# Delta-rule stage of a two-layer decoder kernel: projections and first taps issued ahead of exponentials and transposes

## The chip, the cores and the metric

One core of one Trainium2 chip runs the whole program in one launch. The metric is device time in microseconds (us); lower is better. Engines are named as in the profile: PE is TensorE (matmuls and transposes), ACT is ScalarE, DVE is VectorE, POOL is GpSimd, SP is SyncE, which here issues most DMAs. Each engine runs its own instructions strictly in the order written and waits on semaphores.

## The reference, cut to what matters

The program is a decoder of two layers, each an attention, a cross attention and a mixture. The change lies in one of the six stages, the attention of layer 1, a gated delta rule with 12 heads of 128 (keys, queries) and 32 (values), over 4 sequences of 256 tokens:

```python
q = short_conv(hidden_states @ Wq, conv_wq)     # 4 taps along time, then silu
k = short_conv(hidden_states @ Wk, conv_wk)
v = short_conv(hidden_states @ Wv, conv_wv)
q = l2norm(q.reshape(B, T, H, -1)); k = l2norm(k.reshape(B, T, H, -1))
beta = jax.nn.sigmoid(hidden_states @ Wb)
g = -jnp.exp(A_log) * jax.nn.softplus(hidden_states @ Wa + dt_bias)
# per head, step by step over t:
S = S * jnp.exp(gt); delta = (vt - kt @ S) * bt
S = S + kt[:, None] * delta[None, :]; o = qt @ S
o_n = o * rsqrt(mean(o * o) + eps) * norm_w * silu(hidden_states @ Wg)
return o_n.reshape(B, T, -1) @ Wo
```

The kernel computes the recurrence in two chunks of 128 tokens for each sequence: decay matrices E from cumulated g, products of keys with keys and queries, the inverse of a unit triangular matrix per chunk (first in blocks of 16, then doubled by matmuls), and the state carried from the first chunk to the second.

## The kernel before

`delta_attention` is written by hand with semaphores. Each engine has one loop `for i in span`, i from -1 to 14; I call one pass of it a step. In step i the heads overlap as in a pipeline:

- head a = i+1: its four projections `project(a, 0..3)` on PE (keys for two pairs of sequences, then queries) into the two PSUM banks of `dh_pj`; the first tap of the convolution, `tap0`, on ACT (L1909); the other three, `taps`, on DVE (L2170); `silu` on ACT (L1917) into `dh_back` and `dh_silu`. For the decays: `mask_g` on POOL (L2389), `segment` on PE (L1630), `exp` on ACT (L1921), `mask_e` on POOL (L2399).
- head b = i: `turn(b, 0..3)` transposes on PE (L1642), `copy_k0` (L1926) and `square` (L1931) on ACT, `sums` and scales `d` (L2176 to L2189) on DVE, `scale_e` on POOL (L2350), `k_products` on PE (L1654), `weigh` on DVE (L2205, L2207).
- head i-3: the levels of the inverse (`level4_x` L1670 up to `level6_y` L1719). They read blocks that POOL has solved (`solve`, L2370 and L2372, for two heads at a time in the even steps from 2 on) and that SP takes through DRAM: `dh_Tm` out to `delta_t`, `delta_t` back to `dh_U`. From i = 3.
- head i-4: the chain `solution` (L1735), `state`, `within` (L1753), `carried`. From i = 4.
- steps -1 to 3 also compute v for all heads: `project_v` on PE, `taps_v` on ACT (L1875, 4 instructions of 128x512), `conv_v` on POOL (L2407, 3 instructions), `silu_v`, `turn_v`, `copy_v`. Steps 11 and 12 compute the output gates (`gate`, L1562).

Buffers set the cross waits: `turn(b, 0)` shares a bank of `dh_tp` with `segment(b, 0)`, so it waits for `exp(b, 0)`; `turn(b, 2)` waits for all of `silu(b, ...)` and for `square(b, 0)`; `project` waits for the taps that read its bank. On ACT the exponentials use another function table than silu, so each step has two table loads; a dummy activation, `early` (L2063), brings the silu table back right behind the exponentials.

Of the kernel before, what the change touches and what calls it, by code (L numbers as in the profile page):

```python
# [1339 lines left out]
def delta_attention(nc, env, first, lf, latent, a, blk_a, blk_t, blk_tt):  # L1340
# [6 lines left out]
    with ExitStack() as ctx:  # L1347
# [88 lines left out]
        UO = (0, 32, 0, 32)  # L1436
        span = range(-1, D_H - 1 + LAG_CHAIN)
        ab, dec = bd[:, 0, 0:TILES * 2 * D_H].rearrange("p (t h) -> p t h", t=TILES), bd[:, 1, 0:2 * TILES * D_H].rearrange("p (n x) -> p n x", n=2)
        v_units, v_turns = {-1: (0, 1), 0: (2, 3), 1: (4, 5)}, {1: (0, 1), 2: (2, 3), 3: (4, 5)}
        spare = [x[:].rearrange("p t (n i) -> p (t n i)", n=1) for x in (PT[3], PT[4], AT[3])]  # L1440
        tap_v = lambda n, j: spare[j - 1][:, 512 * (n % 2):512 * (n % 2) + 512].rearrange("p (b t) -> p b t", t=SEQ)
# [3 lines left out]
        with nc.Block() as block:  # L1445
# [75 lines left out]
            def _(pe):  # L1521
# [95 lines left out]
                def project(a, n):  # L1617
                    u, (m, s) = 4 * a + n, divmod(n, 2)
                    if n == 0:
                        pe.wait_ge(w_loaded[a % 2], 32 * (a // 2 + 1))  # L1620
                    need(pe, tapped, 3 * (u - 1))
                    for k in range(KC):
                        mm = pe.matmul(pj[:, n % 2, :], w[a % 2][:, m, k, :], env.xT[:, k, 512 * s:512 * s + 512], start=(k == 0), stop=(k == KC - 1))  # L1623
                    mm.then_inc(projected, 1)
# [143 lines left out]
                for i in span:  # L1768
                    a, b = heads(i + 1), heads(i)
                    news, olds, late, ends = v_units.get(i, ()), v_turns.get(i, ()), gates.get(i, ()), outs.get(i, ())  # L1770
                    if b is not None:
                        turn(b, 0)
                        turn(b, 1)
                    if a is not None:
                        project(a, 0)
                    if i == -1:
                        betas_and_gates()
                    for h in chain_heads(i):
                        solution(h, 0)
                    for l in level_heads(i):  # L1780
                        level4_x(l)
                    for t in late[0:1]:
                        gate(t)
                    if b is not None:
                        turn(b, 2)
                        turn(b, 3)
                    if a is not None:
                        project(a, 1)
                    for n in olds[0:1]:
                        turn_v(n)  # L1790
                    for n in news[0:1]:
                        project_v(n)
                    for q in ends[0:1]:
                        turn_pair(q)
                    for l in level_heads(i):
                        level4_y(l)
                    for h in chain_heads(i):
                        state(h)
                    for t in late[1:2]:
                        gate(t)  # L1800
                    if b is not None:
                        k_products(b, 0)
                        k_products(b, 1)
                    for l in level_heads(i):
                        level5_x(l)
                    for h in chain_heads(i):
                        within(h, 0)
                    for h in chain_heads(i):
                        carried(h)
                    for q in ends[0:1]:  # L1810
                        out_pair(q)
                    for l in level_heads(i):
                        level5_y(l)
                    for h in chain_heads(i):
                        turn_carried(h)
                    if a is not None:
                        project(a, 2)
                    for n in olds[1:2]:
                        turn_v(n)
                    for n in news[1:2]:  # L1820
                        project_v(n)
                    for t in late[2:3]:
                        gate(t)
                    for q in ends[1:2]:
                        turn_pair(q)
                    for h in chain_heads(i):
                        solution(h, 1)
                    for l in level_heads(i):
                        level6_x(l)
                    if b is not None:  # L1830
                        k_products(b, 2)
                        k_products(b, 3)
                    for t in late[3:4]:
                        gate(t)
                    for q in ends[1:2]:
                        out_pair(q)
                    for l in level_heads(i):
                        level6_y(l)
                    for h in chain_heads(i):
                        within(h, 1)  # L1840
                    if i == -1:
                        decays()
                    if a is not None:
                        segment(a, 0)
                        segment(a, 1)
                        project(a, 3)
                for f in range(2):
                    turn_last(f)
                for f in range(2):
# [5 lines left out]
            def _(act):  # L1855
# [63 lines left out]
                def exp(a, c):  # L1919
                    act.wait_ge(seg_done, 2 * a + c + 1)  # L1920
                    act.activation(E[a % 2][c][:], tp[:, c, :].rearrange("p (b i) -> p b i", b=BATCH), ACT.Exp).then_inc(exp_done, 1)  # L1921
# [68 lines left out]
                for i in span:  # L1990
# [4 lines left out]
                    if b is not None:  # L1995
                        copy_k0(b)
                        square(b, 0)
                        square(b, 1)
                    if a is not None:
                        tap0(a, 0)  # L2000
                    if i == -1:
                        act.wait_ge(z_done, 1)
                        act.activation(u_[:], u_[:], ACT.Exp, scale=-1.0).then_inc(u_done, 1)
                        act.activation(par[:, :, B_, :], ab[:, :, 0:D_H].rearrange("p t h -> p h t"), ACT.Sigmoid).then_inc(beta_done, 1)
                    if b is not None:
                        silu(b, 3)
                    for l in level_heads(i):
                        copy_x4(l)
# [49 lines left out]
                    if i == -1:  # L2058
                        exp_decays()
                    if a is not None:  # L2060
                        exp(a, 0)
                        exp(a, 1)
                        act.activation(early[:], env.c("ident")[:, 0:1], ACT.Silu)  # L2063
                        tap0(a, 3)
                    for n in news[1:2]:
                        taps_v(n)
                for f in range(D_H - 2, D_H):
                    square_out(f)
                for f in range(2):
# [273 lines left out]
            def _(pool):  # L2343
# [83 lines left out]
                for i in span:  # L2427
                    a, b, g, f = heads(i + 1), heads(i), group(i), heads(i - LAG_NORM)
                    news = v_units.get(i, ())
                    if b is not None:  # L2430
                        scale_e(b, 0)
                        scale_e(b, 1)
                    if g is not None:
                        eye(g)
                        if g < PAIRS - 1:
                            solve(g)
                            turn_solved(g)
                    if i == D_H:
                        pool.wait_ge(x6_done, 9)
                        pool.memset(AT[0][:], 0.0).then_inc(recleared, 1)  # L2440
                        pool.wait_ge(o_done, 16)
                        pool.memset(PT[2][:, :, 0:64], 0.0).then_inc(recleared, 1)
                    for l in level_heads(i):
                        if l % 4 == 0:
                            pool.wait_ge(v_copied, 2 * (l // 4) + 2)
                        rhs(l)
                    if i == -1:
                        pool.wait_ge(g_done, 1)
                    if a is not None:
                        mask_g(a, 0)  # L2450
                        mask_g(a, 1)
                    for n in news[0:1]:
                        conv_v(n)
                    if b is not None:
                        if i == 0:
                            pool.wait_ge(dec_exp, 1)
                        norms(b)
                    if f is not None:
                        invert_out(f)
                        if f < 8:  # L2460
                            norm_out(f)
                    if a is not None:
                        mask_e(a, 0)
                        mask_e(a, 1)
                    for n in news[1:2]:
                        conv_v(n)
                for f in range(D_H - 2, D_H):
                    invert_out(f)
                pool.wait_ge(half_done, 1)
# [970 lines left out]
```

## Time and profile before

| What | Value |
|---|---|
| median of 3 runs | 1415.07 us (1415.04 to 1422.34) |
| the profiled execution | 1407.76 us, of which the profile's span is 1405.8 us |
| delta stage in the span | 461.9 us to about 860 us |
| busy over the span | PE 91%, DVE 58%, ACT 39%, POOL 37% |
| mean granted TensorE clock | 0.935 of 2.4 GHz |
| step length, first tap to first tap (L1909, last of each step), steps 0 to 4 | 23.9, 24.4, 27.2, 23.7, 25.3 us |
| the same, steps 5 to 10 | 25.3 to 25.4 us each |

The busy share of one engine over the whole span hides that stages differ; the stretches of single steps below are the ones to read. "Idle before" in a row is how long the engine stood still before that row, and the arrow says what ended the wait. A PE row gives the modelled length of its matmuls; the next row's start is the better measure of how long PE was held.

### The profile page before, as it was taken

What the parts mean: (1) busy time and instruction counts of PE and PEld (TensorE: products, weight loads), DVE (VectorE), ACT (ScalarE), POOL (GpSimd) and SP (SyncE); (2) the same over time, 40 slices, a digit from 0 to 9 for tenths busy, and PEclk for the clock granted to TensorE, in tenths of its full rate; (3) what the DMA queues carried; (4) which work ended last, traced back from release to release, by engine and by line L of the source; (5) the groups of instructions that cost most, each with busy time, mean ns of one, the idle gap of its engine ahead of it and who ended that gap; (6) DMA issues with size and microseconds to landing.
All of it is one profiled execution on the core that took longest, in us unless ns stands there. A gap on an engine that the chain in (4) does not pass through costs nothing. (4 is left out here: it accounts for less than half of the span.)

```text
span 1405.8 us, 25099 instructions
## 1 busy us (share of the span) xinstructions
PE 1272.7 (91%) x9172; PEld 842.6 (60%) x9172; DVE 813.6 (58%) x1826; ACT 548.4 (39%) x1273; POOL 523.1 (37%) x597
## 2 busy tenths in 40 slices
PE   7999999847896877999999977799999989999998
PEld 4868778635555444677777766345555555344487
DVE  5464655556354475676776423577777773743343
ACT  4554636233223576767667331144344351000010
POOL 3452627530751367476577301322222201500010
PEclk9999999958898798999999977899999999999999
DMA  3010038533886201212122120100000206542100
GB/s 132 24 37 15 22 108 277 202 125 148 237 251 200 79 11 24 43 31 40 34 38 26 20 43 1 62 20 21 21 22 30 63 1 172 180 139 68 34 8 23
DMA packets 144168, 106.57 MB, mean 76 GB/s; under 512 B 87873, under 2 KB 130089, under 8 KB 142913
## 3 DMA queue, kind: packets, MB, share of 16 engines
q1 hardware_dynamic: 135904, 88.31, 22.0%
q0 software_dynamic: 4496, 13.33, 3.6%
q10 hardware_dynamic: 3664, 3.55, 0.8%
q8 instruction: 66, 1.08, 0.3%
q14 instruction: 38, 0.30, 0.1%
HBM read 84.16 MB, written 22.35 MB: 76 GB/s over the span
## 5 line engine op out<-in xcount | busy, mean ns | idle before, releaser
L2811 PE MATMUL la_banks<-la_xe,la_f_w 128*128 128x512 f32 x348 | 151.4, 593 | 3.5 <-DVE la_xe L3189 3.5
L2170 DVE SCALAR_TENSOR_TENSOR dh_front<-dh_pj,df_conv,dh_front 128x510 f32<-128x510 f32 x144 | 107.4, 746 | 76.2 <-ACT dh_front L1909 72.4
L3352 POOL TENSOR_TENSOR la_area<-la_area 128x512 f32<-128x512 f32 x48 | 60.3, 1277 | 172.4 <-DVE la_area L3032 152.0
L2811 PEld LDWEIGHTS la_banks<-la_xe,la_f_w 128*128 128x128 f32 x348 | 65.4, 190 | 83.6 <-issue 83.6
L346 POOL TENSOR_TENSOR wa_qkT<-lf_area 128x512 f32<-128x512 f32 x40 | 50.7, 1268 | 96.8 <-DVE lf_area L318 96.8
L3189 DVE TENSOR_TENSOR la_xe<-xT,la_area 128x1024 f32<-128x1024 f32 x29 | 52.6, 1830 | 55.5 <-PE la_banks L2811 48.1
L2929 ACT ACTIVATE la_area<-la_banks,la_nmax 128x256 f32<-128x256 f32 x128 | 59.0, 475 | 58.5 <-DVE la_nmax L3041 58.5
L350 POOL TENSOR_TENSOR mw_gu<-mw_gu,const 128x384 f32<-128x384 f32 x64 | 63.6, 999 | 30.0 <-ACT mw_gu L381 30.0
L3372 POOL TENSOR_TENSOR la_o_rstd<-la_o_var,la_minus_half 128x1 f32<-128x1 f32 x8 | 6.4, 803 | 164.3 <-DVE la_o_var L3251 164.3
L2937 ACT COPY la_area<-la_banks 128x512 f32<-128x512 f32 x64 | 37.5, 590 | 56.2 <-PE la_banks L2660 55.9
L273 PE MATMUL wa_po<-wa_wo,mw_rows 128*128 128x256 f32 x256 | 56.6, 379 | 0.0
L2864 PE MATMUL la_banks<-la_y,la_area 128*128 128x256 f32 x256 | 56.2, 379 | 0.0
L3041 DVE TENSOR_REDUCE la_nmax<-la_banks 128x4 f32<-128x1024 f32 x32 | 39.1, 1221 | 26.9 <-PE la_banks L2646 26.7
L2864 PEld LDWEIGHTS la_banks<-la_y,la_area 128*128 128x128 f32 x256 | 48.4, 190 | 6.9 <-issue 0.5
L1623 PE MATMUL dh_pj<-xT,df_w 128*128 128x512 f32 x96 | 49.7, 643 | 2.9 <-PEq L133 2.9
L273 PEld LDWEIGHTS wa_po<-wa_wo,mw_rows 128*128 128x128 f32 x256 | 48.0, 190 | 6.2
L3052 DVE TENSOR_SCALAR la_area<-la_area,la_rec 128x256 f32<-128x256 f32 x128 | 50.3, 454 | 1.1
L318 DVE TENSOR_TENSOR lf_area<-wa_swap,const 128x512 f32<-128x512 f32 x40 | 48.4, 1209 | 0.0
L2613 PE MATMUL la_banks<-xT,lf_area 128*128 128x512 f32 x96 | 45.5, 616 | 2.5 <-PEq L133 2.5
L1623 PE MATMUL dh_pj<-xT,dh_w 128*128 128x512 f32 x96 | 46.7, 609 | 0.0
L2613 PE MATMUL la_banks<-xT,la_area 128*128 128x512 f32 x96 | 44.8, 602 | 0.0
L2660 PEld LDWEIGHTS la_banks<-const,la_area 128*128 128x128 f32 x256 | 28.6, 141 | 25.2 <-issue 22.7
(621 smaller groups left out, 3090.1 us busy)
## 6 DMA issues: line engine op xcount, KB each, us to landing
mw_gu<-in_L_ffn_gate_up SPq DMA_DIRECT2D x16, 768.0 KB, 14.2
placed<-mw_rows SPq DMA_DIRECT2D x8, 768.0 KB, 10.7
mw_d<-in_L_ffn_down SPq DMA_DIRECT2D x16, 384.0 KB, 13.6
mw_rows<-placed SPq DMA_DIRECT2D x8, 768.0 KB, 6.8
la_area<-w_table POOLq DMA_DIRECT2D x6, 1024.0 KB, 12.2
pairs<-me_picked SPq DMA_DIRECT2D x7, 704.0 KB, 3.9
la_f_w<-in_L_ffn_q_proj SPq DMA_DIRECT2D x32, 128.0 KB, 2.2
la_f_w<-in_L_ffn_k_proj SPq DMA_DIRECT2D x32, 128.0 KB, 2.4
```

Of the source, the lines that this page charges most:

```text
L273: mm = pe.matmul(po[:, (t + 1) % 2, 0:DIM], encT[:, i, P * t:P * t + P], wos[:, i, :], start=(i == 0), stop=(i == A_G - 1))
L346: pool.tensor_tensor(qkT[:, m, 512 * c:512 * c + 512], t_cos[:, n % 2, :], t_sin[:, n % 2, :], ALU.add).then_inc(rotated, 1)
L350: pool.tensor_tensor(masked[:, u % 3, :], probs[:, u % 2, :], env.c("a_mask"), ALU.mult).then_inc(mask_done, 1)
L1623: mm = pe.matmul(pj[:, n % 2, :], w[a % 2][:, m, k, :], env.xT[:, k, 512 * s:512 * s + 512], start=(k == 0), stop=(k == KC - 1))
L2170: dve.scalar_tensor_tensor(dst, src[:, :, 0:SEQ - j], conv[:, a, m, D_CONV - 1 - j:D_CONV - j], dst, ALU.mult, ALU.add).then_inc(tapped, 1)
L2613: mm = pe.matmul(qb[:, n, :], wabs[i % 2][:, k, n, :], env.xT[:, k, 512 * c:512 * c + 512], start=(k == 0), stop=(k == KC - 1))
L2811: mm = pe.matmul(acc[c][m], f_w[n % SLOTS][:, m, k, :], xe[(n - U) % RING][:, k, :], start=first and k == 0, stop=last and k == KC - 1)
L2864: mm = pe.matmul(o_acc[t % 4], ae[t % RING][:, x, :], f_wo[:, x, :], start=(x == 0), stop=(x == F_E - 1))
L2929: ins = act.activation(e[:, u % 2, a, n, :], sc[bank(j, b)][:, a, n, :], ACT.Exp, bias=nmax[:, a, t:t + 1], accum_out=total[:, a, t:t + 1])
L3052: ins = dve.tensor_scalar(en[:, u % 2, a, n, :], e[:, u % 2, a, n, :], rec[:, a, 2 * b + n:2 * b + n + 1], None, ALU.mult)
L3189: dve.tensor_tensor(xe[(n - U) % RING][:], env.xT[:, :, HALF * c:HALF * c + HALF], wb[c][:, x:x + 1, :].to_broadcast([P, KC, HALF]), ALU.m ...
L3352: pool.tensor_tensor(qrot[:, c, n, :], prod[:, c, 2 * n, :], prod[:, c, 2 * n + 1, :], ALU.add).then_inc(rotated, 1)
```

## The change

Nothing is added or removed; instructions change place on PE, ACT and POOL; DVE and SP keep their order.

- PE: `project(a, 0)` now comes before `turn(b, 0)` and `turn(b, 1)`; `project(a, 3)` before the two `segment`s.
- ACT: `tap0(a, 3)` comes before the two `exp`s. In steps 0 to 2 (`filling`) `silu(b, 3)` comes before `tap0(a, 0)`; later steps keep it behind. The second `taps_v` of a step moves from its end into the next step, behind `tap0(a, 0)`.
- POOL: the second `conv_v` of a step moves into the next step, behind `scale_e`. In step 2 (`g == 0`) `mask_g` comes before the solve.

```diff
+        filling = lambda i: i < LAG_LEVELS
...
 # PE
+                    if a is not None:
+                        project(a, 0)
                     if b is not None:
                         turn(b, 0)
                         turn(b, 1)
-                    if a is not None:
-                        project(a, 0)
...
                     if a is not None:
+                        project(a, 3)
                         segment(a, 0)
                         segment(a, 1)
-                        project(a, 3)
...
 # ACT
                         square(b, 0)
                         square(b, 1)
+                    if b is not None and filling(i):
+                        silu(b, 3)
                     if a is not None:
                         tap0(a, 0)
+                    for n in v_units.get(i - 1, ())[1:2]:
+                        taps_v(n)
...
-                    if b is not None:
+                    if b is not None and not filling(i):
                         silu(b, 3)
...
                     if a is not None:
+                        tap0(a, 3)
                         exp(a, 0)
                         exp(a, 1)
                         act.activation(early[:], env.c("ident")[:, 0:1], ACT.Silu)
-                        tap0(a, 3)
-                    for n in news[1:2]:
-                        taps_v(n)
...
 # POOL
                         scale_e(b, 0)
                         scale_e(b, 1)
+                    for n in v_units.get(i - 1, ())[1:2]:
+                        conv_v(n)
+                    if a is not None and g == 0:
+                        mask_g(a, 0)
+                        mask_g(a, 1)
                     if g is not None:
                         eye(g)
...
-                    if a is not None:
+                    if a is not None and g != 0:
                         mask_g(a, 0)
                         mask_g(a, 1)
...
-                    for n in news[1:2]:
-                        conv_v(n)
```

The order of the instructions shows it. The changed file has lines shifted by 1 on PE and ACT at these places and by 3 on POOL, so L1623 there is L1624, L1909 is L1910, L2389 is L2392.

PE before, where the step of head a = 6 ends and the next begins (`dh_tp<-dh_E` are the segments, `dh_pj` the projections, `dh_tp<-const` the transposes, `dh_bd<-dh_r` the solution, `dh_lv<-dh_U` level4_x):

```order
L1630 MATMUL dh_tp<-dh_E,const 128x512 x2
L1623 MATMUL dh_pj<-xT,df_w 128x512 x2
L1642 MATMUL dh_tp<-const,dh_back 128x128 x4
L1642 MATMUL dh_tp<-const,dh_silu_0 128x128 x4
L1623 MATMUL dh_pj<-xT,dh_w 128x512 x2
L1735 MATMUL dh_bd<-dh_r,dh_TT 128x32 x4
L1670 MATMUL dh_lv<-dh_U,dh_AT 32x16 x32
L1642 MATMUL dh_tp<-const,dh_back 128x128 x4
```

PE of the change at the same place:

```order
L1624 MATMUL dh_pj<-xT,df_w 128x512 x2
L1631 MATMUL dh_tp<-dh_E,const 128x512 x2
L1624 MATMUL dh_pj<-xT,dh_w 128x512 x2
L1643 MATMUL dh_tp<-const,dh_back 128x128 x4
L1643 MATMUL dh_tp<-const,dh_silu_0 128x128 x4
L1736 MATMUL dh_bd<-dh_r,dh_TT 128x32 x4
L1671 MATMUL dh_lv<-dh_U,dh_AT 32x16 x32
L1643 MATMUL dh_tp<-const,dh_back 128x128 x4
```

Both projections moved up by one group; one of them has left the stretch between the segments and the last row, the transposes of `turn(b, 2)`.

ACT before, at the same seam:

```order
L1965 COPY dh_TT<-dh_lv 64x8x64
L1921 ACT_TABLE_LOAD
L1921 ACTIVATE dh_E<-dh_tp 128x512 x2
L2063 ACT_TABLE_LOAD
L2063 ACTIVATE dh_early<-const 128x1
L1909 ACTIVATE dh_front<-dh_pj,df_conv 128x512
L1926 COPY dh_k_1<-dh_tp 128x512
L1931 ACTIVATE dh_front<-dh_tp 128x512 x2
L1909 ACTIVATE dh_front<-dh_pj,df_conv 128x512
L1917 ACTIVATE dh_back<-dh_front 128x256
```

ACT of the change:

```order
L1966 COPY dh_TT<-dh_lv 64x8x64
L1910 ACTIVATE dh_front<-dh_pj,df_conv 128x512
L1922 ACT_TABLE_LOAD
L1922 ACTIVATE dh_E<-dh_tp 128x512 x2
L2069 ACT_TABLE_LOAD
L2069 ACTIVATE dh_early<-const 128x1
L1927 COPY dh_k_1<-dh_tp 128x512
L1932 ACTIVATE dh_front<-dh_tp 128x512 x2
L1910 ACTIVATE dh_front<-dh_pj,df_conv 128x512
L1918 ACTIVATE dh_back<-dh_front 128x256
```

The first tap stands in front of the exponentials, and in front of the table load that belongs to them.

POOL before, in step 2, from conv_v of unit 5 to the start of the first solve:

```order
L2407 TENSOR_TENSOR lf_area<-lf_area,dh_PT 128x2x255
L2407 TENSOR_TENSOR lf_area<-lf_area,dh_PT 128x2x254
L2407 TENSOR_TENSOR lf_area<-lf_area,dh_AT 128x2x253
L2350 TENSOR_TENSOR dh_back<-dh_E,dh_d 128x512 x2
L2355 MEMSET dh_Tm 128x256
L2357 MEMSET dh_Tm 128x16
L2370 TENSOR_TENSOR dh_tmp<-dh_Ab,dh_Tm 128x15
```

POOL of the change:

```order
L2353 TENSOR_TENSOR dh_back<-dh_E,dh_d 128x512 x2
L2410 TENSOR_TENSOR lf_area<-lf_area,dh_PT 128x2x255
L2410 TENSOR_TENSOR lf_area<-lf_area,dh_PT 128x2x254
L2410 TENSOR_TENSOR lf_area<-lf_area,dh_AT 128x2x253
L2392 TENSOR_TENSOR dh_E<-const,dh_par 128x512 x2
L2358 MEMSET dh_Tm 128x256
L2360 MEMSET dh_Tm 128x16
L2373 TENSOR_TENSOR dh_tmp<-dh_Ab,dh_Tm 128x15
```

conv_v now stands behind scale_e, and mask_g (`dh_E<-const`) ahead of the solve, where it was behind it.

## Rows read from the trace of the kernel before

**Rows 1.** The page's first line.

```profile
span 1405.8 us, 25099 instructions
```

**Rows 2.** Busy time by stretch: steps 1, 2 and 6.

```profile
core 0: us, PE busy (x) PEld busy (x) DVE busy (x) ACT busy (x) POOL busy (x), PEclk, DMA share, GB/s
...
513.52:537.87 24.35, 20.05 (x69) 11.67 (x68) 16.29 (x29) 18.34 (x36) 16.47 (x15) 0.93 0.08 17
537.87:565.10 27.23, 17.57 (x55) 10.16 (x54) 15.62 (x29) 16.13 (x31) 22.03 (x45) 0.81 0.23 33
...
639.45:664.72 25.27, 25.17 (x392) 18.20 (x391) 18.30 (x43) 17.10 (x39) 18.09 (x42) 1.00 0.26 36
```

**Rows 3.** Timeline of ACT where step 2 begins (start, length, idle before).

```profile
538.44 0.68 ACT L1875 ACTIVATE lf_area<-dh_lv,dh_cw 128x512 f32<-128x512 f32 x1
...
540.72 0.61 ACT L1926 COPY dh_k<-dh_tp 128x512 f32<-128x512 f32 x1
541.18 1.13 ACT L1931 ACTIVATE dh_front<-dh_tp 128x512 f32<-128x512 f32 x2
542.15 0.74 ACT L1909 ACTIVATE dh_front<-dh_pj,df_conv 128x512 f32<-128x512 f32 x1
```

**Rows 4.** Timeline of PE, steps 2 to 4.

```profile
543.55 1.12 PE L1642 MATMUL dh_tp<-const,dh_back 128*128 128x128 f32 x4 [4.15 <-ACT dh_silu L1917]
...
559.27 3.78 PE L1630 MATMUL dh_tp<-dh_E,const 128*128 128x512 f32 x4 [5.52 <-POOL dh_E L2389]
...
567.52 0.73 PE L1670 MATMUL dh_lv<-dh_U,dh_AT 32*32 32x16 f32 x64
...
592.67 0.66 PE L1642 MATMUL dh_tp<-const,dh_back 128*128 128x128 f32 x4 [0.57 <-ACT dh_silu L1917]
```

**Rows 5.** Timeline of POOL, step 2.

```profile
540.93 2.42 POOL L2407 TENSOR_TENSOR lf_area<-lf_area,dh_PT 128x510 f32<-128x510 f32 x2 [2.39 <-ACT dh_AT L1875]
...
544.61 2.04 POOL L2350 TENSOR_TENSOR dh_back<-dh_E,dh_d 128x512 f32<-128x512 f32 x2
...
558.18 2.03 POOL L2389 TENSOR_TENSOR dh_E<-const,dh_par 128x512 f32<-128x512 f32 x2
```

**Rows 6.** DMA: the first issue of solved blocks, and the issues' landing time.

```profile
560.97 1.83 SPq L1491 DMA_DIRECT2D dh_U<-delta_t  x4
...
dh_U<-delta_t SPq DMA_DIRECT2D x24, 32.0 KB, 2.1
```

**Rows 7.** Timeline of PE at the seam of steps 6 and 7, and in step 11.

```profile
660.70 1.96 PE L1630 MATMUL dh_tp<-dh_E,const 128*128 128x512 f32 x4
...
665.09 1.88 PE L1623 MATMUL dh_pj<-xT,df_w 128*128 128x512 f32 x4
...
668.54 0.66 PE L1642 MATMUL dh_tp<-const,dh_back 128*128 128x128 f32 x4
...
769.77 0.66 PE L1642 MATMUL dh_tp<-const,dh_back 128*128 128x128 f32 x4 [0.33 <-ACT dh_silu L1917]
```

**Rows 8.** Timeline of ACT at the same seam of steps 6 and 7.

```profile
660.49 1.28 ACT L1921 ACT_TABLE_LOAD   x1
...
662.70 0.60 ACT L1921 ACTIVATE dh_E<-dh_tp 128x512 f32<-128x512 f32 x1 [0.26 <-PE dh_tp L1630]
663.32 1.28 ACT L2063 ACT_TABLE_LOAD   x1
...
664.72 0.67 ACT L1909 ACTIVATE dh_front<-dh_pj,df_conv 128x512 f32<-128x512 f32 x1
665.29 0.58 ACT L1926 COPY dh_k<-dh_tp 128x512 f32<-128x512 f32 x1
665.75 1.10 ACT L1931 ACTIVATE dh_front<-dh_tp 128x512 f32<-128x512 f32 x2
667.01 0.69 ACT L1909 ACTIVATE dh_front<-dh_pj,df_conv 128x512 f32<-128x512 f32 x1 [0.16 <-PE dh_pj L1623]
667.76 0.42 ACT L1917 ACTIVATE dh_back<-dh_front 128x256 f32<-128x256 f32 x1
```

## The prediction

> **What bounds the kernel now.** I read the page's first line for the span [rows 1], then cut the delta stage into steps, from one last first tap (L1909) to the next, and took the busy time of each stretch [rows 2]. They are of two kinds. In steps 0 to 3 no engine is full: step 1 has PE busy 20.05 and ACT 18.34 of 24.35 us, step 2 PE 17.57 of 27.23 us. In steps 5 to 10 PE is busy all but 0.1 us of each, 25.17 of 25.27 us in step 6 [rows 2], at a granted clock of 1.00. Then I read the timelines at the places where instructions move. The reader is to see three waits. PE stands 4.15 us before the transposes of `turn(b, 2)` at the start of step 2 (543.55), because `silu(b, 3)` is queued on ACT behind four `taps_v`, `copy_k0`, two squares and a tap [rows 3, 4]. In step 2 PE stands 5.52 us before the segments, since `mask_g` is queued on POOL behind the whole solve [rows 4, 5]. In the full steps there is no such wait to take: at 668.54 `turn(b, 2)` follows close on what stands before it, and ACT's chain from the segments to it is just as long as PE's work [rows 7, 8].
>
> **The change, part by part.** No instruction is added or removed, so every term is a shift of a wait. I count shifts at fixed marks against the profiled execution: minus is earlier.
>
> *Steps -1 to 1, gain.* At the seam of a fill step ACT runs the four `taps_v` ahead of `copy_k0`, 538.44 to 540.72 = 2.28 us [rows 3]. They go behind the next tap, so the first `copy_k0` comes 2.3 us earlier (`tap0(a, 3)` stays ahead of it in both orders). Within a step `silu(b, 3)` now follows the squares directly and the last tap no longer waits for the exponentials. I laid the same row lengths out again in the new order for steps 0 and 1. From `copy_k0(1)`, in us: squares done 1.4, silu 2.1, tap 2.6, `taps_v` 4.9, squares 5.9, tap 6.5, second `taps_v` done 9.9, third tap 11.4, `silu(2, 2)` 14.4, `silu_v` 15.5, last tap 16.9 (it waits 0.7 for PE), table load, exponentials and table load 20.7, next `copy_k0` 20.8. Step 0 comes out at 20.2 in the same way. ACT's own busy time of 18.34 us [rows 2] is the floor of such a step. They took 23.9 and 24.3 us, so `copy_k0(2)` moves from 540.72 [rows 3] to 531.2: -2.3 - 3.7 - 3.5 = -9.5.
>
> *Step 2, POOL.* `scale_e(2)` follows `d(2)` and starts at 544.61 - 9.5 = 535.1. But two things now stand between it and the solve that did not: `conv_v(5)`, 540.93 to 544.5 = 3.6 us before and ahead of `scale_e`, and `mask_g(3)`, 2.0 us [rows 5]. So the segments lose their wait of 5.52 us, but the solve, and all that hangs on it, moves only by -9.5 + 3.6 + 2.0 = -3.9.
>
> *Step 3, where that stall goes.* What is late next is the solved block. The four `dh_U` loads were issued from 560.97 on, the last at 562.3, and landed 2.1 us later [rows 6], at 564.4; now at 560.5. PE asks for them in `level4_x(0)`, ahead of `turn(3, 2)`, and in the replay it is ready at about 553: a new wait of some 8 us. `level4_x(0)` moves from 567.52 [rows 4] to 560.6, -6.9. After 4.15 us of standing the transposes took 1.12 us against 0.66 [rows 4, 7], and after 5.52 us the segments 3.78 against 1.96 [rows 4, 7]; over the transposes and the projection behind the wait that costs 1.6 us (bounds 0 and 2.0; I take the value of these rows, since the wait is longer than either): -5.3. DVE meanwhile finished work of step 3 that it did later before, which gives 1.2 back, and the seam into step 4 costs 0.9 by the sum below, less what its 0.57 us of waiting covered [rows 4]. -5.3 - 1.2 + 0.9 = -5.6, I carry -5.7: `turn(4, 2)` moves from 592.67 [rows 4] to 587.0. Bounds: -3.5 (cold clock at 2.0, nothing given back) and -9.5 (the blocks never waited for).
>
> *Steps 5 to 11, loss.* From the first segment to `turn(b, 2)` PE did 7.84 us of work (660.70 to 668.54) [rows 7]: segments, `project(a, 3)`, transposes, `project(a+1, 0)`, `solution`, `level4_x`. The order of this work changes, its sum does not, so PE would reach `turn(b, 2)` 7.8 us after the start P of `project(a, 3)`. ACT's chain from P in the new order: the tap starts 1.92 after its projection (665.09 to 667.01) [rows 7, 8]; tap 0.69; table load 1.28; two exponentials at 0.60; table load 1.28; dummy 0.12; `copy_k0` 0.46; squares 1.10; `tap0(a+1, 0)` 0.57; `silu(b, 3)` until the transposes 0.78 (667.76 to 668.54) [rows 7, 8]. Together 9.40; with pairs counted by start to start (0.97 for the squares, 541.18 to 542.15 [rows 3], and 1.09 for the exponentials) 9.16. The difference is the table load: before, the first load ran at 660.49 under PE's work and the second exponential still waited 0.26 us for its segment [rows 8]; now it is queued behind a tap that waits for a projection, while ACT stands. So PE waits 1.3 to 1.6 us at each `turn(b, 2)`; I take 1.4. Behind it are all later PE instructions, and PE has no slack in these steps to win it back. Six seams, b = 5 to 10: 8.4. Into step 11 no `tap0(12, 0)` exists, so ACT's chain is 0.57 shorter: 0.8, on 769.77 [rows 7]. Loss 9.2. DVE gets its first input of the step earlier by the tap, POOL's scales follow it, and neither is reached.
>
> The Trainium skill ("ScalarE: Activation LUTs", What ACT_TABLE_LOAD costs) gives a switch about 1283 ns for the load and 1380 ns more for a drain; this case's load agrees with 1.28 us, but its rows show no drain: the exponential ends at 663.30 and the load starts at 663.32 [rows 8]. By the page's 2.66 us per switch the two switches of a seam would add 2.8 us to the chain, and the sum would be about 19 us more.
>
> *Sum.* -5.7 + 9.2 = +3.5 on the span of 1405.8 [rows 1]: 1409.3, and with the 1.96 us around the span 1411.3 for an execution like the profiled one. The profiled execution (1407.76) lies 7.3 us under the median of the runs shown, 1415.07; carried over to it, 1418.6. I say 1418.5. What a measurement of this kernel tells from no change is about 0.5%, 7 us, so the likeliest case reads as no change.
>
> **The rivals.**
> - *Forecast:* gain in the fill, loss at every full seam, +3.5 (own range -2 to +8, from the bounds above). Chance 0.56.
> - *The full seams cost nothing* because ACT's chain is shorter than I add up: PE's transposes waited less than 0.2 us there, and 1.4 us must vanish. Then -5.7: 1409.4. For it: ACT has 8 us of idle time per step; against it: none of that lies in this chain. 0.11.
> - *The fill keeps all its gain* and the seams cost nothing: -9.5, 1405.6. It needs the solved blocks to come early although POOL has 5.6 us more ahead of the solve. 0.07.
> - *Slower, by the clock:* each new wait at `turn(b, 2)` lets PE fall to 1.2 GHz of its 2.4, as 4.15 us of waiting did [rows 4]. Price 1.6 us per seam, seven seams: +11.2 on top, 1429.8. It decides from the point where a wait of 1.4 us is enough; against it, the wait of 0.57 us left the transposes at 0.66 [rows 4]. 0.09.
> - *Slower, by the fill:* the gain before step 3 is lost at `level4_x(0)`, for instance by the DMAs of the solved blocks queueing behind others. +9.2, 1424.3. 0.08.
> - *Slower, by the table load:* a load behind a tap that reads PSUM is not hidden and holds the queue for as long again as it lasts, 1.28 us [rows 8], at seven seams: +9.0 on top, 1427.6. 0.04. This is near what the page's drain would do for one of the two switches; the trace does not agree with it so far, as said.
> - *Nothing moves* anywhere by more than 1 us, since the waits are held by something that I did not see. 1415. 0.05.
>
> **How the numbers follow.** Below 1408 lie the third case and scatter of the second and the first: 0.12. Over 1422 lie the three slower cases, less a part of the second of them, and the upper end of the forecast's own range: 0.19. The rest, 0.69, is within 0.5%. The range 1407 to 1428 leaves out the third case, the clock case and a little of the others, under 2 in 10.
>
> **What the new profile would show.** The first three steps, last exponential to last exponential, take 20 to 21 us where they took 24 to 27. PE waits for `dh_U` blocks for 7 to 9 us before `level4_x(0)`, and its clock falls there. `mask_g` of step 2 stands before the solve and no segment waits for POOL. In steps 5 to 10 the length is 26.7 us instead of 25.3; ACT stands about 2 us before `tap0(a, 3)`, and PE 1.3 to 1.6 us before each `turn(b, 2)`, released by `silu`. The delta stage's last instruction comes 2 to 5 us later. Wrong would be: full steps still at 25.3 us (then faster by what the fill gives), full steps over 28 us (clock or drain), or `level4_x(0)` at 567 again.

## The result, and the profile after

Ten runs of each kernel: 1427.28 us (1417.7 to 1434.1) against 1415.81 us (1413.33 to 1422.34). The ratio over the runs is 1.0067, interval 1.0047 to 1.0087 (the quotient of the two medians alone would be 1.0081): slower by 0.7%. 1427.28 us is 9 us over the stated 1418.5 and lies inside the stated range, 0.7 us under its upper end.

The page of the changed kernel, its span, its busy time of PE and DVE and the granted clock by slices:

```profile
span 1428.3 us, 25099 instructions
...
PE 1275.8 (89%) x9172; PEld 844.6 (59%) x9172; DVE 813.7 (57%) x1826; ACT 544.3 (38%) x1273; POOL 521.1 (36%) x597
...
PEclk9999999858698799899999968799999999999999
```

The span is 22.5 us longer than [rows 1], but not all of that is the change. The delta stage's first projection starts at 473.89 us here and at 461.92 before, and what runs ahead of it is the same program. Over the traces of this study that start lies anywhere from 458.7 to 480.7 us, without relation to the edits (the last value belongs to one of the fastest kernels below). It goes in part with the chip: 458.7 to 462.9 in the six traces from one chip (e1 to e4, e9, e10), 469.1 to 480.7 in the four from another (e5 to e8). So I count within the stage, between three marks on PE: `turn(0, 0)`, the first transposes of step 0; `turn(4, 2)`, where the fill is over; and `turn(11, 2)`. The start of the stage up to `turn(0, 0)` is left out, since its length changes with the granted clock: 22.5 us at 0.84 in e2 and 26.6 us at 0.69 in e10, two of the runs below. `turn(0, 0)` starts here, before and changed, and the last two marks of the changed kernel follow; those of before are in [rows 4] and [rows 7].

```profile
487.85 0.63 PE L1642 MATMUL dh_tp<-const,dh_back 128*128 128x128 f32 x4 [1.78 <-ACT dh_E L1921]
...
499.69 0.63 PE L1643 MATMUL dh_tp<-const,dh_back 128*128 128x128 f32 x4 [1.52 <-ACT dh_E L1922]
...
598.59 0.66 PE L1643 MATMUL dh_tp<-const,dh_back 128*128 128x128 f32 x4 [1.56 <-ACT dh_silu L1918]
...
791.38 0.66 PE L1643 MATMUL dh_tp<-const,dh_back 128*128 128x128 f32 x4
```

| | fill: turn(0,0) to turn(4,2) | full steps: turn(4,2) to turn(11,2) |
|---|---|---|
| before | 104.8 us | 177.1 us |
| changed | 98.9 us | 192.8 us |

The fill gained 5.9 us and the full steps lost 15.7 us: +9.8. With the start of the stage, 12.0 us later, that makes 21.8 of the 22.5 us.

PE of the changed kernel at a full seam, the end of step 7 and the start of step 8 (start, length, idle before; lines are shifted by one):

```profile
699.43 1.96 PE L1624 MATMUL dh_pj<-xT,df_w 128*128 128x512 f32 x4
701.23 1.88 PE L1631 MATMUL dh_tp<-dh_E,const 128*128 128x512 f32 x4
702.95 1.88 PE L1624 MATMUL dh_pj<-xT,dh_w 128*128 128x512 f32 x4
...
708.73 1.12 PE L1643 MATMUL dh_tp<-const,dh_back 128*128 128x128 f32 x4 [1.56 <-ACT dh_silu L1918]
709.64 1.06 PE L1643 MATMUL dh_tp<-const,dh_silu 128*128 128x128 f32 x4
710.49 2.70 PE L1624 MATMUL dh_pj<-xT,dh_w 128*128 128x512 f32 x4
```

ACT over the same stretch:

```profile
701.43 0.69 ACT L1910 ACTIVATE dh_front<-dh_pj,df_conv 128x512 f32<-128x512 f32 x1 [2.23 <-PE dh_pj L1624]
702.14 1.28 ACT L1922 ACT_TABLE_LOAD   x1
703.43 1.08 ACT L1922 ACTIVATE dh_E<-dh_tp 128x512 f32<-128x512 f32 x2
704.53 1.28 ACT L2069 ACT_TABLE_LOAD   x1
705.83 0.20 ACT L2069 ACTIVATE dh_early<-const 128x1 f32<-128x1 f32 x1
705.94 0.57 ACT L1927 COPY dh_k<-dh_tp 128x512 f32<-128x512 f32 x1
706.40 1.09 ACT L1932 ACTIVATE dh_front<-dh_tp 128x512 f32<-128x512 f32 x2
707.37 0.70 ACT L1910 ACTIVATE dh_front<-dh_pj,df_conv 128x512 f32<-128x512 f32 x1
707.94 0.43 ACT L1918 ACTIVATE dh_back<-dh_front 128x256 f32<-128x256 f32 x1
```

Read the two together. ACT stands 2.23 us for the projection, and only then comes the table load that ran under PE's work in [rows 8]. From there to the silu there is no gap on ACT. PE has nothing left to do and stands 1.56 us, where [rows 7] show none. A wait of 1.56 us stands before `turn(b, 2)` at each of the seven seams from step 4 to step 10. At the seam behind them, into step 11, PE waits at `turn(11, 0)` instead, for the exponential:

```profile
787.40 0.63 PE L1643 MATMUL dh_tp<-const,dh_back 128*128 128x128 f32 x4 [1.06 <-ACT dh_E L1922]
```

The step lengths of the changed kernel, from one dummy activation to the next, steps 5 to 8 and step 10, with the granted clock (PEclk, third number from the end):

```profile
624.10:652.38 28.28, 26.72 (x393) 19.33 (x392) 18.96 (x43) 16.76 (x38) 12.48 (x12) 0.94 0.18 30
652.38:679.10 26.72, 25.16 (x393) 18.20 (x392) 18.45 (x43) 16.65 (x37) 21.46 (x45) 1.00 0.21 27
679.10:705.83 26.73, 25.17 (x393) 18.20 (x392) 18.86 (x43) 16.65 (x38) 12.46 (x12) 1.00 0.23 41
705.83:734.20 28.37, 26.81 (x393) 19.33 (x392) 18.87 (x43) 16.76 (x38) 21.64 (x45) 0.94 0.23 34
...
760.92:789.05 28.13, 25.51 (x392) 18.88 (x392) 18.48 (x43) 16.77 (x37) 21.56 (x45) 0.94 0.20 26
```

26.7 us is the forecast step, 1.4 us over the step before (a wait of 1.56 us costs a little less than its length, because PE stood 0.1 us of each step before, too). In 28.3 us the same wait was followed by PE at its lower clock: at 708.73 the transposes take 1.12 us and the projection 2.70 instead of 0.66 and 1.88 [rows 7]. The wait is the same 1.56 us in both kinds of step.

PE in the fill, steps 0, 1 and 3:

```profile
503.67 0.94 PE L1643 MATMUL dh_tp<-const,dh_back 128*128 128x128 f32 x4 [2.86 <-ACT dh_silu L1918]
...
525.24 0.66 PE L1643 MATMUL dh_tp<-const,dh_back 128*128 128x128 f32 x4 [2.45 <-ACT dh_silu L1918]
...
572.32 1.05 PE L1671 MATMUL dh_lv<-dh_U,dh_AT 32*32 32x16 f32 x64 [9.51 <-DMA dh_U<-delta_t]
573.30 1.11 PE L1643 MATMUL dh_tp<-const,dh_back 128*128 128x128 f32 x4
```

The waits for silu are shorter than the 4.15 us of [rows 4] and the wait for POOL is gone; in its place PE stands 9.51 us for the solved blocks.

### The profile page after: what moved, and what is told of

It reads as the page before. It is cut to its first block and busy times, and to the rows that moved or that the text cites. A ratio compares the mean times of both kernels' runs of the same rounds, so it can differ in the third digit from the quotient of the medians.

```text
span 1428.3 us, 25099 instructions
## 1 busy us (share of the span) xinstructions
PE 1275.8 (89%) x9172; PEld 844.6 (59%) x9172; DVE 813.7 (57%) x1826; ACT 544.3 (38%) x1273; POOL 521.1 (36%) x597
## 5 line engine op out<-in xcount | busy, mean ns | idle before, releaser
L3047 DVE TENSOR_REDUCE la_nmax<-la_banks 128x4 f32<-128x1024 f32 x32 | 39.1, 1221 | 26.9 <-PE la_banks L2652 26.7
L1624 PE MATMUL dh_pj<-xT,df_w 128*128 128x512 f32 x96 | 49.9, 645 | 2.9 <-PEq L133 2.9
L2179 DVE TENSOR_REDUCE dh_ss<-dh_front 128x4 f32<-128x512 f32 x48 | 30.7, 679 | 35.5 <-ACT dh_front L1932 28.0
L1624 PE MATMUL dh_pj<-xT,dh_w 128*128 128x512 f32 x96 | 49.6, 642 | 0.0
L2402 POOL TENSOR_TENSOR dh_E<-dh_E,const 128x512 f32<-128x512 f32 x24 | 30.0, 1269 | 49.8 <-ACT dh_E L1922 49.8
## 6 DMA issues: line engine op xcount, KB each, us to landing
la_area<-w_table POOLq DMA_DIRECT2D x6, 1024.0 KB, 11.3
```

## The experiments

All ratios are to the kernel before, measured on the same chip in turns. `LAG_LEVELS` is 3. The marks come from one profiled execution of each kernel, and single clock falls in the fill move them by 1 to 2 us each; the ratios come from 5 to 12 executions. Where an expectation gives marks from the first projection, I compare differences between marks in the table behind the experiments.

**The new order only in the fill (e1).** PE and ACT keep the old order at the end of step 3 and later.

```diff
                     if a is not None:
-                        project(a, 3)
+                        if i < LAG_LEVELS:
+                            project(a, 3)
                         segment(a, 0)
                         segment(a, 1)
+                        if not (i < LAG_LEVELS):
+                            project(a, 3)
```

and likewise `tap0(a, 3)` on ACT, and `project(a, 0)` with `i <= LAG_LEVELS`.

> The new order only in the fill (PE's and ACT's seams up to step 3, POOL as changed), the old order in the full steps. I count from the stage's first projection to the transposes turn(4, 2) and turn(11, 2): before 130.8 and 307.9 us, changed 124.7 and 317.5. My theory: the changed kernel lost only at the full seams (1.56 us of waiting at each, and PE's fall to the half clock behind some of them) and gained 5 to 6 us in the fill. Then full steps are back at 25.3 us, turn(4, 2) comes at 123.5 to 124.7, turn(11, 2) at about 301.4, and the time is 6 us under before (ratio 0.995 to 0.997). Rival: the loss sits in the fill or ahead of the stage (the changed profile had 12 us more ahead of it) and the seams only show it; then the time stays at or above before, ratio 1.00 to 1.007.

Measured: ratio 0.9968, 0.9948 to 0.9988. Fill 98.0 us, full steps 177.1 us. PE at the seam of steps 6 and 7:

```profile
651.04 0.60 PE L1643 MATMUL dh_tp<-const,dh_back 128*128 128x128 f32 x4
655.36 0.66 PE L1643 MATMUL dh_tp<-const,dh_back 128*128 128x128 f32 x4
```

No wait is left before the second row. The loss was at the full seams; the rival falls. The ratio lies in the expected 0.995 to 0.997.

**The new order only in the full steps (e2).** The reverse: `filling` never true, `taps_v`, `conv_v` and `mask_g` at their old places, the new order of PE and ACT from the end of step 3 on.

> The new order only from the end of step 3 on, the fill as before. Theory: no gain and the whole loss, 1.4 us per seam and 1.6 us more where the clock falls: steps of 26.7 and 28.3 us, turn(4, 2) at about 131.7, turn(11, 2) at about 324, time 16 us over before (ratio 1.009 to 1.013). Rival that the loss comes from the fill: ratio near 1.000, steps of 25.3 us.

Measured: ratio 1.0108, 1.0085 to 1.0131. Fill 106.8 us, full steps 192.7 us, with the wait of 1.56 us at each seam:

```profile
620.25 1.11 PE L1643 MATMUL dh_tp<-const,dh_back 128*128 128x128 f32 x4 [1.56 <-ACT dh_silu L1923]
```

Both halves apart make the whole to within 1 us: -6.8 and +2.0 in the fill, 0.0 and +15.6 in the full steps, against -5.9 and +15.7 together. The 2.0 us that this one loses in the fill hold its first new seam, into step 4.

**silu first in all steps (e3).**

```diff
-        filling = lambda i: i < LAG_LEVELS
+        filling = lambda i: True
```

> The changed kernel with silu(b, 3) ahead of tap0(a, 0) in all steps and not only in steps 0 to 2: ACT's chain to turn(b, 2) gets shorter by that tap, 0.57 us. Theory: the wait at turn(b, 2) falls from 1.56 to 1.0 us, full steps to 26.1 us where the clock holds; turn(11, 2) at 314 if the clock falls as often as in the changed kernel, at 307.5 if a wait of 1.0 us never lets it fall. Ratio to before 0.999 to 1.004. Rival, the wait is not ACT's chain but the segments or the exponentials themselves: steps stay at 26.7 to 28.3 us and the ratio at 1.007.

Measured: ratio 1.0054, 1.0033 to 1.0075. PE at two seams:

```profile
618.36 0.66 PE L1643 MATMUL dh_tp<-const,dh_back 128*128 128x128 f32 x4 [0.99 <-ACT dh_silu L1918]
...
646.20 1.11 PE L1643 MATMUL dh_tp<-const,dh_back 128*128 128x128 f32 x4 [0.98 <-ACT dh_silu L1918]
```

The wait fell by 0.57 us, exactly the tap that went out of the chain. The clock did not hold at the shorter wait: four of the seven steps between the marks take 27.8 us, the others 26.2. I had left that open in the expectation, and the ratio came out over the stated 1.004; its interval reaches down to 1.0033.

**Only project(a, 0) ahead, in the full steps (e4).** The fill as in e1; `project(a, 3)` and `tap0(a, 3)` old from the end of step 3 on, `project(a, 0)` always ahead of the transposes.

> Fill as changed; in the full steps only project(a, 0) stands ahead of the transposes, project(a, 3) and tap0(a, 3) stay behind the segments and the exponentials. Theory: copy_k0 comes later by the projection that is now ahead of its transposes (1.72 us less slack), and the chain copy_k0, squares, tap, silu makes PE wait about 1.0 us at turn(b, 2): steps of 26.2 us, turn(11, 2) at about 307, ratio 0.999. Rival: only the first tap ahead of the table load costs anything, and this part is free: steps of 25.3 us, turn(11, 2) at 301.4, ratio 0.996.

Measured: ratio 1.0053, 1.0033 to 1.0073. The wait before `turn(b, 2)` is 0.94 us at each seam, five of the seven steps take 25.3 to 26.1 us, and two take 27.8 with the lower clock:

```profile
612.71 0.70 PE L1643 MATMUL dh_tp<-const,dh_back 128*128 128x128 f32 x4 [0.94 <-ACT dh_silu L1921]
...
640.51 0.66 PE L1643 MATMUL dh_tp<-const,dh_back 128*128 128x128 f32 x4 [0.94 <-ACT dh_silu L1921]
```

The wait is the expected one, but the ratio is not the expected 0.999: two falls of the clock and a fill of 101.0 us, 3.0 us over e1, stand against it. The rival, that this part is free, falls.

**Only project(a, 3) and its tap ahead, in the full steps (e5).** The other half.

> Fill as changed; in the full steps only project(a, 3) and tap0(a, 3) stand ahead of the segments and the exponentials, project(a, 0) stays behind the transposes. Theory: the exponentials come later by the tap and the uncovered table load, while PE has only the segments to do before turn(b, 0): it waits about 1.1 us there for exp and 0.2 us at turn(b, 2), so steps are 26.6 us as with the whole change, turn(11, 2) near 310.6, ratio about 1.002. Rival: the loss needs the other projection too, steps of 25.3 us, ratio 0.996.

Measured: ratio 1.0053, 1.0028 to 1.0078 (1.002 expected); steps of 26.7 us, all at a granted clock of 1.00.

```profile
644.35 0.63 PE L1643 MATMUL dh_tp<-const,dh_back 128*128 128x128 f32 x4 [1.06 <-ACT dh_E L1924]
...
648.91 0.66 PE L1643 MATMUL dh_tp<-const,dh_back 128*128 128x128 f32 x4 [0.26 <-ACT dh_silu L1920]
```

Its step 5, in the same columns as the step lengths above:

```profile
619.29:646.01 26.72, 25.41 (x391) 18.10 (x390) 18.87 (x43) 16.65 (x37) 12.46 (x12) 1.00 0.23 42
```

The waits stand where they were expected, 1.06 us for the exponential at `turn(b, 0)` and 0.26 us at `turn(b, 2)`. Against the 25.3 us of before, and where the clock holds, a step is 0.8 us longer with `project(a, 0)` alone (e4), 1.4 with `project(a, 3)` and its tap alone (e5), and 1.4 with both (changed). They do not add, because both delay the same chain on ACT. The full steps of e5 are 9.4 us longer than before without one fall of the clock.

**The table load under the wait (e6).** As e3, and from step 3 on a dummy exponential ahead of the tap:

```diff
                     if a is not None:
+                        if i >= LAG_LEVELS:
+                            act.activation(sooner[:], env.c("ident")[:, 0:1], ACT.Exp)
                         tap0(a, 3)
```

> The changed kernel with silu(b, 3) first in all steps, and from step 3 on a dummy exponential of one column ahead of tap0(a, 3), so that the table load runs while ACT stands waiting for the projection. Theory: the exponentials start when their segments are done, 0.7 us earlier, and with silu first the chain is 1.27 us shorter: PE waits 0.3 us at turn(b, 2), steps of 25.5 us, no fall of the clock, turn(11, 2) at 303 to 305, ratio 0.996 to 0.998. Rival: if the load is not what makes the chain long, the steps stay at 26.1 us as with silu first alone.

Measured: ratio 0.9959, 0.9936 to 0.9982; fill 99.5 us, full steps 178.6 us. ACT and PE at one seam:

```profile
645.05 1.28 ACT L2067 ACT_TABLE_LOAD   x1
646.34 0.20 ACT L2067 ACTIVATE dh_sooner<-const 128x1 f32<-128x1 f32 x1
...
648.97 0.60 ACT L1922 ACTIVATE dh_E<-dh_tp 128x512 f32<-128x512 f32 x1 [0.26 <-PE dh_tp L1631]
649.59 1.28 ACT L2071 ACT_TABLE_LOAD   x1
```

```profile
653.36 0.66 PE L1643 MATMUL dh_tp<-const,dh_back 128*128 128x128 f32 x4 [0.36 <-ACT dh_silu L1918]
```

The second exponential waits 0.26 us for its segment again, as in [rows 8], and PE's wait is down from 0.98 us to 0.36. One dummy instruction took 0.62 us out of every full step. With it the full steps of the new order are only 1.5 us longer in all than those of the old (178.6 against 177.1), and its fill is 5.3 us shorter (99.5 against 104.8): the kernel is faster than before, with the new order in all steps.

**A longer chain (e7).** The changed kernel with three activations of 128 columns more behind the second table load.

> The changed kernel with three dummy activations of 128 columns on ACT behind the table load of each seam from step 3 on, about 0.6 us in all. If ACT's chain is what PE waits for, the wait at turn(b, 2) grows from 1.56 to about 2.2 us and each full step by 0.6 us. If a longer wait lets the clock fall at every seam instead of at every second, each costs 1.6 us more: steps of 28.9 us, turn(11, 2) at 326; if not, 321.7. Rival, PE waits for something else: steps stay at 26.7 and 28.3 us.

Measured: ratio 1.0056, 1.0035 to 1.0076.

```profile
649.08 0.69 ACT L2073 ACTIVATE dh_longer<-const 128x128 f32<-128x128 f32 x3
```

```profile
652.47 0.66 PE L1644 MATMUL dh_tp<-const,dh_back 128*128 128x128 f32 x4 [2.15 <-ACT dh_silu L1919]
```

The next instruction, `copy_k0`, starts 0.60 us behind these three's start, and PE's wait grew by 0.59 us (1.56 to 2.15). Each step is 27.3 us long, and the clock fell at none of the seams from step 4 to 10. The full steps took 190.7 us, less than the changed kernel's 192.8 with its shorter wait. The chain is shown; I had expected the clock to fall at least as often as in the changed kernel, and that was wrong.

**conv_v(5) behind the solve (e8).** As e1, with the head's last `conv_v` taken from the steps before and put behind the first solved group, and its `silu_v(5)` on ACT in step 3 behind `tap0(a, 0)`:

```diff
-        v_silus = {0: (0, 1), 1: (2, 3), 2: (4, 5)}
+        v_silus = {0: (0, 1), 1: (2, 3), 2: (4,)}
...
-                    for n in v_units.get(i - 1, ())[1:2]:
+                    for n in (v_units.get(i - 1, ())[1:2] if i < 2 else ()):
...
                             turn_solved(g)
+                        if g == 0:
+                            conv_v(5)
```

> As the kernel with the new order in the fill only, and conv_v(5) goes behind the first solve and its copy on POOL, silu_v(5) on ACT into step 3 behind its first tap. Theory: the wait of 9.5 us for the solved blocks before level4_x(0) is set by POOL's queue ahead of the solve, which loses 3.6 us of it: wait of about 6 us, turn(4, 2) and turn(11, 2) 3.6 us earlier than with the fill alone (120.4 and 297.8), ratio 0.993 to 0.995. Rival: the wait is the DMAs' own, and nothing moves.

Measured: ratio 0.9923, 0.9896 to 0.9951 (0.993 to 0.995 expected). The wait is down from 9.46 us (e1) to 5.97:

```profile
554.10 1.05 PE L1671 MATMUL dh_lv<-dh_U,dh_AT 32*32 32x16 f32 x64 [9.46 <-DMA dh_U<-delta_t]
...
574.47 1.05 PE L1671 MATMUL dh_lv<-dh_U,dh_AT 32*32 32x16 f32 x64 [5.97 <-DMA dh_U<-delta_t]
...
577.22 3.43 PE L1624 MATMUL dh_pj<-xT,df_w 128*128 128x512 f32 x4
```

POOL's queue ahead of the solve sets that wait, as claimed. The fill shows only 0.8 us of it (97.2 against 98.0), since this execution had PE at the lower clock twice more: in step 1 (22.3 us from `turn(1, 0)` to `turn(2, 0)` against 20.8 in e1) and at 577.22, where the projection took 3.43 us against 2.25 in e1.

**mask_g(3) ahead of the exponentials of step 1 (e9).** As e8, with `mask_g(3, 0)` and `mask_g(3, 1)` at the end of step 1 on POOL, ahead of `mask_e(2)`.

> As the run with conv_v(5) behind the first solve, and mask_g(3) stands on POOL at the end of step 1, ahead of mask_e(2), where POOL waited 1.5 us for the exponentials. Theory: the solve has 2.0 us less ahead of it, so PE's wait before level4_x(0) falls from 6.0 to about 4 us, turn(4, 2) comes 1 to 2 us earlier, and what hangs on the clock behind that wait may get better. Ratio 0.991 to 0.993. Rival: the wait is no longer set by the solve, and nothing moves.

Measured: ratio 0.9948, 0.9928 to 0.9968; the expected 0.991 to 0.993 was missed. Its interval overlaps that of e8, the two were not run on the same chip, and I do not rank them. In the one profiled execution the fill took 93.5 us, 11.3 us under before, which is more than the ratio shows (0.52% is 7.3 us). The wait:

```profile
549.03 1.05 PE L1671 MATMUL dh_lv<-dh_U,dh_AT 32*32 32x16 f32 x64 [4.67 <-DMA dh_U<-delta_t]
```

It fell by 1.3 us against e8, while 2.0 us of work left the queue; where the rest went was not looked into.

**mask_g(3) back behind the solve (e10).** As e1, with `mask_g` in step 2 where it was.

> The kernel with the new order in the fill only, but mask_g(3) back behind the first solve, as before the change. My theory is that the 5.5 us of waiting that the move of mask_g took from the segments came back as the wait for the solved blocks, so that this part of the change is worth nothing: with mask_g behind it the solve ends 2.0 us earlier, PE waits some 7 us for the segments again and hardly for the blocks (0 to 3 us), and level4_x(0) and turn(4, 2) come within 1.5 us of the run with the fill alone. Ratio 0.996 to 0.998. Rival: the move of mask_g is what the fill gains by, turn(4, 2) comes 4 to 5 us later, ratio 1.000.

Measured: ratio 0.9957, 0.9942 to 0.9972 (0.996 to 0.998 expected); fill 96.8 us, 1.2 us less than e1.

```profile
550.89 3.48 PE L1631 MATMUL dh_tp<-dh_E,const 128*128 128x512 f32 x4 [7.08 <-POOL dh_E L2400]
...
556.90 0.73 PE L1671 MATMUL dh_lv<-dh_U,dh_AT 32*32 32x16 f32 x64
```

The wait of 7.08 us is back before the segments and there is none for the blocks. Moving `mask_g` ahead of the solve only changed what PE waits for.

| Kernel | fill, us | full steps, us | wait at a full seam, us | ratio |
|---|---|---|---|---|
| before | 104.8 | 177.1 | none | 1 |
| changed | 98.9 | 192.8 | 1.56 | 1.0067 |
| e1 fill only | 98.0 | 177.1 | none | 0.9968 |
| e2 full steps only | 106.8 | 192.7 | 1.56 | 1.0108 |
| e3 silu first | 102.8 | 189.8 | 0.98 | 1.0054 |
| e4 project(a, 0) | 101.0 | 185.3 | 0.94 | 1.0053 |
| e5 project(a, 3), tap | 100.6 | 186.5 | 1.06 + 0.26 | 1.0053 |
| e6 silu first, load early | 99.5 | 178.6 | 0.36 | 0.9959 |
| e7 longer chain | 101.3 | 190.7 | 2.15 | 1.0056 |
| e8 conv_v(5) | 97.2 | 177.1 | none | 0.9923 |
| e9 and mask_g(3) | 93.5 | 177.1 | none | 0.9948 |
| e10 mask_g old | 96.8 | 177.1 | none | 0.9957 |

## Why the prediction was right or wrong

**Fill, gain at turn(4, 2).** Forecast -5.7, measured -5.9, counted from `turn(0, 0)`; e1, with the same order in the fill but for the seam into step 4, has -6.8. Windows of the changed kernel over steps 0 and 1 (us, then busy time of PE, PEld, DVE, ACT and POOL, PEclk, DMA share, GB/s):

```profile
501.35:522.92 21.57, 19.12 (x60) 11.13 (x60) 15.44 (x30) 17.24 (x33) 16.45 (x15) 0.92 0.09 18
522.92:543.69 20.77, 18.32 (x68) 10.83 (x68) 15.56 (x29) 17.99 (x35) 16.42 (x15) 1.00 0.10 20
```

Counted in the same way, the first solve came 4.0 us earlier (3.9 forecast) and `level4_x(0)` 7.0 us (6.9 forecast). Steps 0 and 1 took 21.6 and 20.8 us from one dummy activation to the next (20.2 and 20.8 forecast; the first ran at a granted clock of 0.92), and `level4_x(0)` waited 9.51 us (some 8). From `level4_x(0)` to `turn(4, 2)` 1.1 us were lost, where the forecast's terms lose 1.3; no row shows the term of 1.2 us that DVE was to give back. With these terms the sum is -5.6, carried as -5.7. The solve was found as the next thing late, and e8 and e10 show it: less ahead of it shortens the wait by as much, and the wait simply changes its name when `mask_g` is put back.

**Full seams, the wait.** Forecast 1.4 us from a chain between 9.16 and 9.40 us, with 1.3 to 1.6 as bounds; measured 1.56. The mechanism is shown from four sides: taking the tap out of the chain took 0.57 us off the wait (e3), covering the table load 0.62 us more (e6), adding 0.59 us put 0.59 us on it (e7), and taking the order back took all of it (e1). The steps of 26.7 us came out as forecast. The term of 9.2 us was right too: e5, whose steps at the full clock are as long as those of the changed kernel (26.7 us), lost 9.4 us in the full steps. Only the place of the last wait was wrong, 1.06 us at `turn(11, 0)` and not 0.8 at `turn(11, 2)`.

**The clock.** This is the step that failed: "each new wait at `turn(b, 2)` lets PE fall to 1.2 GHz" had a chance of 0.09 and a price of +11.2 for seven seams, and was no part of the sum. Between the marks three of the six steps that end in a wait of 1.56 us took 28.3 to 28.4 us and three took 26.7, so the price of a step was right, 1.6 us, and its count was not nothing. The last step took 27.6 us, with a granted clock of 0.94, against 26.2 in e3 and e5, where it has the same wait of 1.06 us at the full clock. Of 192.8 - 177.1 = 15.7 us the waits explain 9.4 (what e5 lost) and four falls of the clock the other 6.3. That is what separates the forecast of +3.5 from +9.8. My own sign of being wrong, full steps over 28 us, came true for these steps. My argument against it, that a wait of 0.57 us left the clock alone, said nothing on a wait of 1.5 us.

**Table load.** No drain appeared: an exponential ends at 704.51 and the load starts at 704.53. The chain was 9.3 us from the start of the projection (699.43 to 708.73), within the bounds taken from rows; the rival built on a load that holds the queue twice as long falls, although its 1427.6 us is the time nearest to the measured 1427.3, and so does, for this place, the 2.66 us per switch of the Trainium skill ("ScalarE: Activation LUTs", What ACT_TABLE_LOAD costs).

**Base.** I carried the forecast from the profiled execution to the median. The stage's start moved by 12 us between the two profiled executions of before and changed, by up to 4 and 12 us among those of one chip, and by 22 us over all, with the same program ahead of it. So the spans of two profiles cannot be compared here; the marks within the stage can, and so can many paired runs. Of the 8.8 us between 1418.5 and 1427.3 the clock explains 6.3; 0.7 is the median of before, 1415.8 and not 1415.1 in the ten runs, and the remaining 1.8 us are less than half the width of the interval (0.4%, 5.7 us).

**Chances and luck.** I gave 0.69 to within 0.5%; the measured 0.67% lies outside, where I gave 0.19, and its interval of 0.47 to 0.87% only just reaches back over the bound. That the time lies in the stated range is in part luck: the range ended at 1428 so as to leave out the clock case of 1429.8, and four falls of seven brought the time to 0.7 us under that end.

## What to carry to other kernels

Read the fill and the full steps apart and apply an order only where its wait exists: the same edit was worth 6.8 us in the fill and cost 15.6 in the full steps. When work moves ahead of a meeting of two engines, count what is left between the meeting points on both, with what stands in each queue behind the instruction that waits: ACT's tap held back a table load of 1.28 us that PE's work had hidden before, and a one-column dummy activation ahead of the tap took 0.62 us of it out again. Before crediting the removal of a wait, ask what else is late: `mask_g` ahead of the solve was worth nothing, while less work ahead of the solve shortened the wait.

## What the runs showed of the hardware that I had not expected

Whether PE falls to its lower clock after a wait did not follow the length of the wait. Waits of 2.15 us at every full seam never did it (e7, clock 1.00 in steps 5 to 10), waits of 1.56 us did at some seams, and waits of 0.98 and 0.94 us at some too (e3 and e4); where it happened it cost 1.4 to 1.7 us. Within one kernel identical steps came out at 26.7 or 28.3 us. The length of the step does not decide it alone either: the steps of e5 are as long as those of the changed kernel, 26.7 us, but wait twice, 1.06 and 0.26 us, and none of them fell. One execution each of e2 and of the changed kernel, which have the same order in the full steps, have their four falls in the same steps, 4, 5, 8 and 10; that speaks against plain chance. What decides is open.
